# Two layers with a routed expert layer: weight conversion moved into the expert loop, experts ranked by load, one scale for all expert inputs

## The reference, cut to what matters

```python
x = x + _L0_ffn_ref(_L0_cond_ref(x, ids0, ...), ...)       # 256 -> 704 -> 256, fake-quantized
h = _L1_cond_ref(x, ids1, W1, b1, W2, b2, gamma, beta)      # adapter, layer norm, gamma and beta of the batch
probs = softmax(h @ Wr); topk_w, topk_idx = top_k(probs, 2) # 9 experts, weights normalized to sum 1
gate = silu(einsum('th,ehi->tei', h, Wg))                   # 256 -> 704
hidden = gate * einsum('th,ehi->tei', h, Wu)
x = x + einsum('tei,eih,te->th', hidden, Wd, cw)            # 704 -> 256
```

## Time and profile before

| | |
|---|---|
| median of three runs | 803.83 us |
| the profiled execution | 805.9 us, its span 804.1 us |
| PE busy | 672.1 us (84%) |
| DVE, ACT, POOL busy | 647.7, 449.8, 288.6 us |
| mean granted TensorE clock | 0.857 |
| front of layer 0 | 0 to 76.4 us |
| gate and up of layer 0 | 76.4 to 145.2 us |
| S loop and tables | 145.2 to 354.3 us |
| expert loop | 354.3 to 804.1 us |

### The profile page before, as it was taken

The page is one execution under the profiler, slowest core; times in us unless marked ns, Lnnn a source line. Parts: engine busy times, 40 slices in busy tenths (PEclk is TensorE's granted clock), DMA queues, the critical chain, the costliest instruction groups (busy, mean ns, idle before and its releaser), DMA issues.

```text
span 804.1 us, 16215 instructions
## 1 busy us (share of the span) xinstructions
PE 672.1 (84%) x4260; PEld 428.0 (53%) x4264; DVE 647.7 (81%) x1881; ACT 449.8 (56%) x801; POOL 288.6 (36%) x262
## 2 busy tenths in 40 slices
PE   6784876588877876219999999999999999999993
PEld 1212332354554545206767767776777767677762
DVE  6687888688999987837888888888888888888862
ACT  2675887578666645115555556555565655556540
POOL 1000455054688887720223222222322223232222
PEclk9665898578678665559999999999999999999996
DMA  6795112244566646863668677566666776766662
GB/s 211 267 363 192 62 37 75 66 151 144 173 192 186 184 141 189 260 223 65 104 103 114 105 99 121 101 114 106 112 108 96 114 104 111 114 104 107 109 89 38
DMA packets 163207, 107.63 MB, mean 134 GB/s; under 512 B 112940, under 2 KB 153012, under 8 KB 163124
## 3 DMA queue, kind: packets, MB, share of 16 engines
q1 hardware_dynamic: 149108, 88.10, 46.3%
q0 software_dynamic: 13440, 17.97, 12.8%
q10 hardware_dynamic: 576, 0.53, 0.2%
HBM read 50.31 MB, written 30.30 MB: 100 GB/s over the span
## 4 chain that ended last, share of the span: by engine, by line
PE 40%; issue 8%; DMA 6%; DVE 1%; POOLq 1%; ACT 1%; SPq 1%; POOL 0%; DVEq 0%; ACTq 0%
PE ps L1036 25%; PE ps L1078 13%; DMA out<-small 4%; PE ps L1020 2%; DMA rows<-small 1%; POOLq L1103 1%; POOL out L1096 0%; DVE small L1047 0%; SPq L972 0%; ACT small L1052 0%; DMA small<-rows 0%; ACT small L1060 0%; POOLq L73 0%; SPq L973 0%; DVE small L1066 0%
## 5 line engine op out<-in xcount | busy, mean ns | idle before, releaser
L1036 PE MATMUL ps<-big,small 128*128 x1728 | 273.2, 315 | 1.6 <-ACT small L1042 1.0
L1096 POOL DMA_INDIRECT out<-small x72 | 111.9, 1554 | 337.2 <-DVE small L1092 295.5
L1036 PEld LDWEIGHTS ps<-big,small 128*128 128x128 f16 x1728 | 164.0, 98 | 93.1 <-issue 2.6
L1078 PE MATMUL ps<-big,small 128*128 (+1 forms) x1224 | 156.4, 277 | 4.7 <-DVE small L1092 4.7
L1052 ACT ACTIVATE small<-small 128x704 f16<-128x704 f32 x72 | 56.9, 790 | 169.0 <-DVE small L1047 169.0
L1078 PEld LDWEIGHTS ps<-big,small 128*128 128x128 f16 (+1 forms) x1224 | 117.7, 99 | 34.3 <-issue 21.2
L1066 DVE SCALAR_TENSOR_TENSOR small<-small 128x64 f16<-128x64 f32 (+1 forms) x144 | 77.8, 582 | 18.8 <-ACT small L1060 18.8
L1047 DVE SCALAR_TENSOR_TENSOR small<-ps,small 128x704 f32<-128x704 f32 x72 | 68.5, 951 | 18.8 <-PE ps L1036 18.8
L858 POOL DMA_INDIRECT rows<-small x64 | 73.5, 1148 | 19.9 <-issue 16.7
L1060 ACT ACTIVATE small<-small 128x704 f16<-128x704 f32 x72 | 63.5, 882 | 16.2 <-DVE small L322 16.2
L609 PE MATMUL ps<-small 128*128 128x512 bf16 x188 | 50.2, 428 | 15.5 <-DVE small L585 9.0
(11 more groups left out here) (156 smaller groups left out, 1038.5 us busy)
## 6 DMA issues: line engine op xcount, KB each, us to landing
small<-rows SPq DMA_DIRECT2D x72, 130.0 KB, 2.1
big<-in_Wg SPq DMA_DIRECT2D x9, 704.0 KB, 4.2
big<-in_Wu SPq DMA_DIRECT2D x9, 704.0 KB, 4.2
big<-in_Wd SPq DMA_DIRECT2D x9, 640.0 KB, 8.2
halves<-big SPq DMA_DIRECT2D x6, 704.0 KB, 4.0
small<-in_xT SPq DMA_DIRECT2D x8, 512.0 KB, 4.0
small<-in_x SPq DMA_DIRECT2D x16, 256.0 KB, 4.1
out<-big SPq DMA_DIRECT2D x16, 256.0 KB, 4.2
```

Source lines behind the costliest of these rows:

```text
L1036: m = put("pe", ("gate", "up")[j], [tk["xsT", t], free, *wload, hl["hi", 26], hl["lo", 26]], lambda e, h=h, k=k, xp=xp, wp=wp, n=n: e.matm ...
L1078: tk["dn", t] = put("pe", "dn", [tk["hT", t], mk("yw", t - 1)], lambda e, n=n, w=w, hc_=hc_, wp=wp, c=c: e.matmul(ps[:, 7, 0:H], hTE[t % 3 ...
L1096: tk["add", t] = dma("pool", f"add{t % 2}", [tk["yw", t], *out_ready], lambda e: e.indirect_dma_start(out=out[:, :], out_offset=bass.Indir ...
```

## The change

- Experts are ranked. After six of eight batches are routed, `st_perm` sorts the experts by their rows so far, largest first; tables and weights follow that rank. By six batches' counts, rank k can't be reached before tile ceil(16k/3).
- No conversion in layer 0, no `halves` tensor, no `load_expert`. The pieces of ranks 0 and 1 (`AHEAD = 6`) are loaded and converted in the last iterations of the S loop and behind the tables. The other 21 are converted inside the expert loop, one per two tiles, loaded by DMAs that ACT issues. The first matmul of tile t waits for those ranks that it may reach.
- The rows of layer 1 are scaled once, by a power of two from the largest |gamma| and |beta|, before they are scattered (a new chain "xb" ahead of the S loop, a scale on the variance term, `scale_beta` on ACT). So `x_bound` and `x_scale` of each tile go, and `x_hi` is a copy.
- `weigh` moves from three DVE to four POOL instructions. `silu` writes into `hid`, and `times` works in place.
- The buffers: `xs` 9 to 6, `xh` 3 to 2. Rows are loaded 3 tiles ahead, not 5.

```diff
-        xs = [carve(small, a, [PAY]) for _ in range(9)]
-        xh = [carve(small, a, [2, H], F16) for _ in range(3)]
+        xs = [carve(small, a, [PAY]) for _ in range(6)]
+        xh = [carve(small, a, [2, H], F16) for _ in range(2)]
...
+        def half_sum(n, waits=()):
+            m = put("act", "hsum", [hl["in", n], *waits], lambda e: e.activation(
+                halves_out(n)[0], slot_in(n), ACT.Square, accum_out=col(wsum, n)))
+            hl["sum", n] = put("act", "hsum", [m], lambda e: e.activation(col(wsb, n), col(wsum, n), ACT.Copy))
...
+        kgb = None
+        for r, v in enumerate((gam, bet)):
+            kgb = dma("sp", "gb", l0, lambda e, r=r, v=v: e.dma_start(gb[0:80, r, :], v.rearrange("a (u n) -> (a u) n", n=32)))
+        m = put("dve", "xb", [kgb], lambda e: e.tensor_reduce(xsc[0:80, 0:2], gb[0:80], AX, ALU.max, apply_absolute_value=True))
...
+            if i == 17:
+                st_perm()
+                for n in range(AHEAD + 2):
+                    half_load(n)
...
         def load_rows(t):
...
-                return e.dma_start(xs[t % 9], Xs[bass.ds(v, P), :])
-            tk["xs", t] = dma("sp", f"xs{t % 9}", [tab, *rows_ready, mk("add", t - 9)], rows)
+                return e.dma_start(xs[t % 6], Xs[bass.ds(v, P), :])
+            tk["xs", t] = dma("sp", f"xs{t % 6}", [tab_row, *rows_ready, mk("add", t - 6)], rows)
...
         def x_hi(t):
-            tk["xhi", t] = put("act", "xhi", [mk("xsc", t)], lambda e: e.activation(
-                xh[t % 3][:, 0, :], xs[t % 9][:, 0:H], ACT.Copy, scale=xc[t % 6][:, 2:3]))
+            tk["xhi", t] = put("act", "xhi", [mk("xs", t), mk("xp", t - 2)], lambda e: e.activation(
+                xh[t % 2][:, 0, :], xs[t % 6][:, 0:H], ACT.Copy))
...
+        begin = {n: 2 * (n - AHEAD) for n in range(AHEAD, 3 * E - 3)}
+        begin.update({3 * E - 3: 36, 3 * E - 2: 39, 3 * E - 1: 42})
...
             on(1, times)
-            on(-2, x_scale)
             on(1, h_bound)
+            on(-2, x_hi)
             on(1, h_scale)
-            on(-2, x_hi)
             on(1, h_hi)
+            piece(1, half_scale, 5)
+            piece(1, unscale)
 
             on(0, lambda t: proj(t, 0, mk("sg", t - 1)))
             on(0, silu)
+            piece(1, half_hi)
+            piece(0, half_sum, [hl["lo", AHEAD - 1]])
             on(-1, turn_rows)
+            on(-2, x_lo)
             on(-1, evac_rows)
-            on(-2, x_lo)
             on(1, h_lo)
             on(3, weigh)
             on(3, down)
             on(3, finish)
-            on(-3, x_bound)
+            piece(2, half_lo)
             on(0, lambda t: proj(t, 1, mk("hid", t - 1)))
-            on(-5, load_rows)
+            piece(0, half_top, 5)
+            on(-3, load_rows)
             on(1, turn_hid)
+            piece(2, lambda n: half_load(n + 2, "act") if n + 2 < 3 * E - 3 else None)
```

More of the change, by code:

```diff
@@ L283, in halves_out @@
[L283 to L316, removed]
+            o = k * EW + j * I
@@ new lines, in halves_out, with half_load, load @@
+            hi, lo = bigf[:, o:o + w], bigf[:, o + EW // 2:o + EW // 2 + w]
+            return hi.bitcast(F16), lo.bitcast(F16)
+        def half_load(n, eng="sp"):
+            k, j = divmod(n, 3)
+            v, nm = slot_in(n), f"hp{n}" if n < AHEAD else f"hl{n % 2 if k < E - 1 else 2}"
+            def load(e):
+                x_ = bass.ds(expert(e, eng, k), 1)
+                if j < 2:
+                    return e.dma_start(v, (Wg, Wu)[j][x_].rearrange("a p n -> p (a n)"))
+                s_ = q.sems[nm]
+                v3 = v.rearrange("p (c n) -> p c n", c=6)
+                e.dma_start(v3[:, 0:5, :], Wd[x_, 0:640].rearrange("a (c p) n -> p (a c) n", p=P)).then_inc(s_, 16)
+                e.dma_start(v3[0:64, 5, :], Wd[x_, 640:704].rearrange("a p n -> p (a n)")).then_inc(s_, 16)
+                return e.dma_start(v3[64:128, 5, :], Wd[x_, 640:704].rearrange("a p n -> p (a n)"))
+            if j == 2:
+                if nm not in q.sems:
+                    q.sems[nm] = ctx.enter_context(nc.semaphore("s_" + nm))
+                    q.count[nm] = 0
+                q.count[nm] += 32
+            if n < AHEAD:
+                free = tk["hq", S - 1]
+            elif k < E - 1:
+                free = hl["lo", n - 2] if n >= AHEAD + 2 else None
+            else:
+                free = hl["lo", n - 1] if j else tk["rows"]
+            hl["in", n] = dma(eng, nm, [tk["perm"], free], load)
@@ L318, in pow2, with half_top @@
+        def half_top(n, bank, waits=()):
+            hl["top", n] = put("pe", "htopp", [hl["sum", n], hl.get(("sc", n - 1)), *waits], lambda e: e.matmul(
+                ps[:, bank, 0:1], onesb, col(wsb, n), start=True, stop=True))
         def pow2(name, waits, top, un, scl):
@@ L322, in pow2, with half_scale, half_hi @@
             return put("dve", name, [m], lambda e: e.reciprocal(scl, un))
[L324 to L342, removed]
+        def half_scale(n, bank):
+            un = col(wun, n)
+            m = put("dve", "hsc", [hl["top", n]], lambda e: e.tensor_scalar(
+                un.bitcast(I32), ps[:, bank, 0:1].bitcast(I32), 1, EXPO, ALU.logical_shift_right, ALU.bitwise_and))
+            m = put("dve", "hsc", [m], lambda e: e.tensor_scalar(un, un, 2.0 ** -113, 2.0 ** 49, ALU.max, ALU.mult))
+            hl["sc", n] = m = put("dve", "hsc", [m], lambda e: e.reciprocal(col(wsc, n), un))
+            if n % 3 < 2:
+                hl["x", n] = put("dve", "hsc", [tk["xun"]], lambda e: e.tensor_scalar(col(wunx, n), un, xsc[:, 4:5], None, ALU.mult))
+        def half_hi(n):
+            hl["hi", n] = put("act", "hhi", [hl["sc", n]], lambda e: e.activation(
                 halves_out(n)[0], slot_in(n), ACT.Copy, scale=col(wsc, n)))
         def half_lo(n):
-            e_, j = pieces[n]
-            w = PW[j]
+            w = PW[n % 3]
             hi, lo = halves_out(n)
@@ L634, in build_program @@
                 pooled4 = pooled
-                if b == 0 and c == 3:
-                    for k in stages[0]:
-                        half_hi(k)
-                    for k in stages[0]:
-                        half_lo(k)
             for c0, c1, o in ((0, 6, b),) if b < NB - 1 else ((4, 6, NB),):
@@ L883, in build_program @@
             at(0, st_hy)
-            piece(0, half_sum, [])
             at(2, st_px)
@@ L890, in build_program @@
             at(2, st_relu)
-            if i < S:
-                piece(2, half_lo)
-                piece(1, half_scale)
             at(3, st_nrm)
             at(4, st_lnT)
-            if 0 <= i - 1 < 27 - EARLY and i < S:
-                half_hi(EARLY + i - 1, [zone_free(EARLY + i - 1)])
+            piece(1, half_scale, 7)
+            piece(1, half_hi)
+            if i % 2 == 0 and 2 <= i < 2 * NB + 2:
+                scale_beta(i // 2 - 1)
             at(2, st_ad)
@@ L920, in build_program @@
             at(2, st_xst)
-            if EARLY + i + 1 >= EARLY + 3 and EARLY + i + 1 < 27:
-                half_load(EARLY + i + 1, [hl["hi", EARLY + i - 2], hl["lo", EARLY + i - 2]])
-            while scattered and parts and i >= parts[0][3]:
-                e_, a, z, _, after = parts.pop(0)
-                load_expert(e_, a, z, [scattered.pop(0), *(tk[k, S - 1] if k in ("hq", "y", "xst", "pd", "x1") else hl[k]
-                                                           for k in after)])
             scattered.clear()
@@ L933, in build_program @@
         last = NB - 1
-        assert not parts
         cond_done = [tk["route", last], tk["lg", S - 1], tk["rk", last], tk["ex", last], tk["lnT", S - 1],
@@ L1027, in build_program, with converted @@
         off = {}
+        def converted(t, j):
+            return [hl[w, 3 * k + j] for k in range(E) if -(-16 * k // 3) <= t for w in ("hi", "lo")]
         def proj(t, j, free):
@@ L1105, in after_turn @@
                 e.wait_ge(q.sems[name], value)
-        for t in range(5):
+        for t in range(3):
             load_rows(t)
         for t in range(2):
-            x_bound(t)
-            x_scale(t)
             x_hi(t)
```

274 lines of the change are left out of this document (135 added, 139 removed).

## The result

The changed kernel takes 1104.0 us (median of four runs, 1098.03 to 1115.73) against 804.02: 1.371 times the time before, 95% interval 1.360 to 1.381. The forecast was 1084, with 1000 to 1180. A run more than 1.5% above the fastest of its kernel counts as slow and stays out of every ratio here: the one of 1115.73 us, the one of 846.1 us of e1_seven and two of the ten of e7_top.

What follows compares the result with a forecast made beforehand. PE was taken to bound the expert loop at 5.87 us a tile, until a ring of row buffers replaced it. From 804.1 us: -30 ahead of the loop, +290 ring, +20 piece transfers, giving 1084 us, range 1000 to 1180.

Steps and rivals of the forecast that it cites:

- The ring: Expert loop: add, row load, x_hi, h_lo and finish form a circle, one 10.26 us turn per tile; +290 us.
- The add leg: Expert loop: from add issued to row load issued, SP's read of the row number included, 4.8 us.
- The page's figure: Skill page's estimate for a 128 KB GpSimd transfer, 2.3 us; by it add leg 2.8, turn 8.3, term +160 us.
- The pieces: Expert loop: 21 conversions cost no compute, but their 704 KB transfers delay adds by 1.0 us each; +20 us.
- Weigh on POOL: Expert loop: four tiny POOL operations behind the add of the tile before end well ahead of finish; cost 0.
- Ahead of the loop: Front -12, first half of S loop -11, its rest -12, new "xb" chain +5; together -30 us.
- The cover that I named for the last conversions: Between tables and first row load: st_perm and six pieces fall in 20 us of waiting for POOL's scatters; without it +7.
- The rivals: Other outcomes, among them PE at half clock throughout the expert loop, 11.74 us a tile: 1161 us, chance 0.06.
- The two-tile ring: Expert loop: finish not behind the late rows, so a 14.2 us turn serves two tiles: 875 us, chance 0.05.
- The faster case: At load_rows: add and row load return within 2.6 us, the ring is hidden, PE stays the bound: 774 us, chance 0.08.
- fit under PE: Expert loop: even without the ring, the conversions' ACT and DVE work fits within PE's 5.87 us a tile.
- The signs: Expert loop: PE about half busy, clock below 1, adds 10 us apart, SP waiting about 4 us, start near 324 us.

Runs made afterwards that it cites:

- e1_seven: The changed kernel with 7 row buffers in place of 6, so a row load waits for the add of t-4, not t-3; 829.6 and 846.1 us.
- e7_top: e2 with PE's tiny matmul half_top moved behind the gate matmuls of the next iteration; 797.0 us, ratio 0.989 to the kernel before.
- e5: The changed kernel with most words of 16 pieces not loaded, conversion passes and DMA issues kept; 1074.6 us.
- e6: The changed kernel with the low parts of the loop's 21 pieces set to zero by a DVE memset, loads kept whole; 1085.0 us.
- e3: The changed kernel with x_hi moved behind silu and half_sum on ACT, and x_lo behind finish and half_lo on DVE; 897.6 and 902.5 us.
- e4: The kernel before with 7 row buffers in place of 9 and rows loaded 4 tiles ahead, not 5; 853.5 us, ratio 1.060.
- e8: e7_top with the loop's piece loads issued by SP in place of ACT; 782.2 us, ratio 0.972 to the kernel before.
- e2: The changed kernel with POOL copying out the row number, so the row load waits for that copy, not the landed add; 808.9 us, ratio 1.005.
- e9: e8 with six unscale operations put behind the first tile's rows and piece 24 loaded in iteration 2; 783.7 us, ratio 0.971.

## Why the prediction was right

The mechanism and its place were right. The size of the sum was right in part by luck: the term of the ring came out too large, that of the pieces too small, and the two errors cancel.

- **The ring.** Forecast 10.26 us a turn, measured 9.94 in the mean of the 46 turns without a piece. 66 turns x (9.94 - 5.87) are some 268 us, where the forecast had 290. The add leg was 4.89 (forecast 4.8), the rows 2.06 (2.20), `x_hi` to `finish` 2.76 (2.98). The reading that the transpose is over before the next add held: it lands 3.7 us in the median after issue. The adds' own landing fell from 5.1 in the median to 3.9. The lower end of 9.4 was a slip: its legs add up to 9.56; nothing hung on it.
- **The page's figure** of the Trainium skill would have made the term +160 in place of +290, and it came out at 268. No run here shows an accumulating add landing in less than 3.7 us, so for this kind of transfer the trace was the better guide.
- **The pieces.** The most mis-sized term. 20 of the 66 turns held a low part and took 12.51 us in the mean, 2.6 more than the others (2.9 where the transfer ran beside it too): 51 us in place of 20. It failed twice: the transfer cost 1.8, near its upper bound of 1.9, and the collision of DVE's pass with POOL's DMA instruction was not in the sum at all. The Trainium skill ("GPSIMD Engine Reference", the table of its specification) says that GpSimd shares its SBUF interface with VectorE and contends with instructions of two SBUF inputs; e5 and e6 agree with it, 2.8 to 3.0 us against 1.63. With the 268 us of the ring this makes 319, and 319.7 were measured from the first add to the 67th.
- **Weigh on POOL.** 0 was right inside the ring. Each tile's four operations took 0.88, 0.29, 0.25 and 0.37 us, and were over 6 us before the next `finish` (604.86 and 610.93).
- **Ahead of the loop.** Forecast -30, measured -33.5: front -18.5 (forecast -12), gate and up 68.7 against 68.8 us (0), the S loop with tables 194.2 against 209.1, -14.9 (-18).
- **Left out:** 5.5 us between the first row load and the first add. The cover that I named for the last conversions, 20 us, was not enough: DVE ran them and six unscale operations until 325.8, while the first rows were there at 322.9.
- **The rivals.** PE was granted 0.81 to 0.84 in the loop and never became the bound: it was busy 7.6 us a turn (498.4 us in 66 turns) in place of 5.87, still below the ring. The two-tile ring is what e3 and e4 built, at 6.5 us a tile in both (e3 behind its pieces; forecast for the rival: 7.1). The faster case is e8: 782 against 774 us named for it. That the conversions would "fit under PE" was too simple: with the ring gone and nothing else moved (e2) the kernel still took 809 us, since PE and ACT stood behind waits in their own lists.
- **The signs.** Adds 10 us apart (10.7 with the pieces), the clock below 1, the late start of the loop (320.8 us for 324) and `x_hi`'s wait for the rows (253.8 / 46, 5.5 us a tile) held. Two were off: PE was busy 69 to 73% and not about half, for the clock; SP waited 8.1 us a tile and not 4, since its wait spans the way to `finish` as well as the add. POOL's wait for `finish`, 7.4 us, is longer than `x_hi`'s.

Not settled: why e1_seven's two runs lie 2% apart, and how much of the 5.5 us at the start of the loop is the late DVE work, which e9 removed without a gain that can be measured.

## What to carry to other kernels

Before a ring of buffers is shortened, write down for one iteration which completion frees the slot, which instruction first reads it, and what stands behind that instruction on every engine up to the one that frees the next slot; if the circle closes, its length over the tiles it serves in one turn is the new period, however idle the engines are. A wait that costs nothing today (SP's 3.0 us a tile) says that something hides it; ask whether the change keeps that slack. Here a copy of one word per row was enough to take the longest completion out of the circle. Where an in-order engine must wait for a small result, ask also what stands behind the wait: register reads and DMA issues lose their cover with it.

## What the runs showed of the hardware

- POOL's indirect DMA instruction took 1.63 us where no low-part pass ran beside it, and 2.81 or 2.95 us where DVE's subtraction with two SBUF inputs (128x1408 or 128x1536) had begun 0.36 us before: it ended 1.5 us behind the pass in all 20 places. In e9 one add missed the pass and took 1.66 us, and one that began 0.73 us after the pass took 2.61. Beside a DVE memset it stayed at 1.63 us.
- An accumulating indirect add of 128 KB landed in 3.9 us in the median in the changed kernel, whose transposes are issued after the add has landed, against 5.1 before, where one is issued about when the add is (569.76 and 569.23 us). No run isolates the transpose as the cause. Without the 704 KB load beside it a turn was 1.8 us shorter (e5).
- With PE busy 69 to 73% of the time in bursts, the granted clock was 0.81 to 0.84, a mean between the levels of 1.2 and 2.4 GHz; in e8, with PE busy 99% from 351.9 to 744.2 us, it was 1.00.
